# Splitting a weight's high part between ScalarE and GpSimd in a per-sequence-weight FFN kernel

## The reference, cut to what matters

```python
def _L0_cond_ref(x, cat_ids, W, b):
    selected_W = W[cat_ids]
    selected_b = b[cat_ids]
    out = jnp.einsum('bsd,bdh->bsh', x, selected_W) + selected_b[:, None, :]
    return out

def _L0_ffn_ref(x, weight):
    w_scale = jnp.mean(jnp.abs(weight)) + EPS
    u = weight / w_scale
    w_quant = u + jax.lax.stop_gradient(jnp.clip(jnp.round(u), -1.0, 1.0) - u)
    a_scale = jnp.max(jnp.abs(x), axis=-1, keepdims=True) + EPS
    z = jnp.clip(x / a_scale * 127.0, -128.0, 127.0)
    a_quant = z + jax.lax.stop_gradient(jnp.round(z) - z)
    y = jnp.einsum('bsi,oi->bso', a_quant, w_quant)
    y = y * (w_scale * a_scale / 127.0)
    return y
x = x + _L0_ffn_ref(_L0_cond_ref(x, itok_B_0_63, L0_cond_W, L0_cond_b), L0_ffn_weight)
```

## Time and profile before

| what | value |
|---|---|
| median of 3 runs | 501.2 us (500.35 to 503.22) |
| the profiled execution: device time | 501.51 us |
| the profiled execution: span in the trace | 499.5 us |
| TensorE busy | 489.8 us, 98% of the span |
| VectorE busy | 371.3 us, 74% |
| ScalarE busy | 333.4 us, 67% |
| GpSimd busy | 305.9 us, 61% |
| DMA | 172.69 MB, mean 346 GB/s |
| granted TensorE clock | full speed in all 40 slices |

### The profile page before, as it was taken

One profiled execution on the slowest core, in us unless ns is written; L12 is line 12 of the kernel. 1 busy time (PEld: TensorE's weight loads), 2 busy tenths in 40 slices (PEclk: granted clock), 3 DMA queues, 4 the chain that ended last, 5 costly groups with the idle time before them and its releaser, 6 DMA issues.

```text
span 499.5 us, 13165 instructions
## 1 busy us (share of the span) xinstructions
PE 489.8 (98%) x2216; PEld 359.5 (72%) x2217; DVE 371.3 (74%) x653; ACT 333.4 (67%) x503; POOL 305.9 (61%) x399
## 2 busy tenths in 40 slices
PE   8889999999999999999999999999999999999996
PEld 3667777777777777777777777767777777777774
DVE  6658776588866797978757879875989587566844
ACT  3666866677758668868656687666767767567642
POOL 7776665655755656666656656565656665655650
PEclk9999999999999999999999999999999999999999
DMA  7879998999989999999999899979999999799953
GB/s 238 271 265 409 412 302 299 363 364 353 414 292 393 380 413 413 410 404 410 335 305 362 299 406 412 403 273 377 412 382 391 383 387 339 247 359 345 318 160 127
DMA packets 71730, 172.69 MB, mean 346 GB/s; under 512 B 8097, under 2 KB 8354, under 8 KB 71586
## 3 DMA queue, kind: packets, MB, share of 16 engines
q1 hardware_dynamic: 53858, 140.01, 76.4%
q10 hardware_dynamic: 17856, 32.51, 17.4%
HBM read 138.94 MB, written 33.55 MB: 345 GB/s over the span
## 4 chain that ended last, share of the span: by engine, by line
PE 88%; DVE 3%; issue 2%; DMA 2%; POOL 1%; DVEq 1%; SPq 1%; ACT 1%; ACTq 1%; POOLq 0%
PE ps_cond L728 22%; PE ps_cond L730 22%; PE ps_cond L729 21%; PE ps_y L681 20%; PE ps_aT L692 2%; DMA sb_w_raw<-cond_wb 2%; DVE sb_w_lo L566 1%; PE ps_cond L655 1%; DVEq L181 1%; DVE sb_absmax L612 1%; POOL sb_xT_hi L350 0%; POOL sb_xT_lo L355 0%; POOL sb_y_scale L380 0%; ACT sb_aT L467 0%; PE ps_cond L646 0%
## 5 line engine op out<-in xcount | busy, mean ns | idle before, releaser
L355 POOL TENSOR_TENSOR sb_xT_lo<-sb_xT_raw,sb_xT_hi 128x512 fp32r<-128x512 f32 x128 | 191.0, 1492 | 156.7 <-PE ps_cond L730 155.1
L728 PE MATMUL ps_cond<-sb_w_hi,sb_xT_hi 128*128 (+1 forms) x512 | 225.1, 440 | 1.3 <-POOL sb_xT_lo L355 1.3
L730 PE MATMUL ps_cond<-sb_w_hi,sb_xT_lo 128*128 (+1 forms) x512 | 201.4, 393 | 0.0
L729 PE MATMUL ps_cond<-sb_w_lo,sb_xT_hi 128*128 (+1 forms) x512 | 199.4, 389 | 0.0
L612 DVE TENSOR_REDUCE sb_absmax<-ps_cond 128x1 f32<-128x512 f32 x128 | 87.7, 685 | 105.3 <-PE ps_cond L730 98.0
L566 DVE TENSOR_TENSOR sb_w_lo<-sb_w_raw,sb_w_hi x106 | 147.2, 1427 | 0.0
L400 ACT ACTIVATE ps_cond<-sb_w_raw 128x512 f32 x127 | 75.8, 597 | 86.7 <-issue 54.8
L681 PE MATMUL ps_y<-sb_ffnT,sb_aT 128*128 128x512 bf16 x508 | 130.2, 379 | 2.5 <-ACT sb_aT L467 2.4
L486 ACT ACTIVATE sb_a_rounded<-ps_cond,sb_a_inv 128x512 int8<-128x512 f32 x128 | 87.7, 685 | 52.3 <-DVE sb_a_inv L618 51.7
L728 PEld LDWEIGHTS ps_cond<-sb_w_hi,sb_xT_hi 128*128 128x128 f32 x512 | 96.3, 188 | 32.5 <-issue 2.4
L730 PEld LDWEIGHTS ps_cond<-sb_w_hi,sb_xT_lo 128*128 128x128 f32 x512 | 96.1, 188 | 22.4
(11 more groups left out here) (86 smaller groups left out, 46.0 us busy)
## 6 DMA issues: line engine op xcount, KB each, us to landing
sb_w_raw<-cond_wb SPq DMA_DIRECT2D x53, 768.0 KB, 7.4
sb_xT_raw<-x_t SPq DMA_DIRECT2D x128, 256.0 KB, 5.7
sb_x_rows<-x SPq DMA_DIRECT2D x128, 256.0 KB, 5.8
out<-sb_x_rows ACTq DMA_DIRECT2D x124, 256.0 KB, 5.6
sb_w_raw<-cond_wb SPq DMA_DIRECT2D x53, 512.0 KB, 5.4
sb_w_raw<-cond_wb SPq DMA_DIRECT2D x5, 256.0 KB, 3.8
sb_ffn_raw<-ffn_t SPq DMA_DIRECT2D x1, 1024.0 KB, 7.5
out<-sb_x_rows SPq DMA_DIRECT2D x3, 256.0 KB, 2.3
```

The costliest lines, as they stand in the source:

```text
L355: pool.tensor_tensor(xT_lo[:, m, :], xT_raw[:, m, :], xT_hi[:, m, :].bitcast(F32), ALU.subtract).then_inc(x_lo_done, 1)
L728: pe.matmul(ps_cond, x_hi_k, w_hi_k, start=(start and k == 0), stop=False, skip_group_check=True)
L729: pe.matmul(ps_cond, x_hi_k, w_lo_k, start=False, stop=False, skip_group_check=True)
L730: last_mm = pe.matmul(ps_cond, x_lo_k, w_hi_k, start=False, stop=(k == KD - 1), skip_group_check=True)
```

## The change

Of a new step's `w_hi` (2048 columns) ScalarE now makes the first three quarters: its second piece shrinks from 1024 to 512 columns. GpSimd makes the last 512 columns, at the end of its step `r` for step `r+4`, behind `x_hi`. For that it waits for the second DMA of the weight, and it needs the table: it looks up a row at the head of each step, and branches. At the start it does this for steps 1, 2 and 3 ahead of its first step. VectorE's second piece of `w_lo` waits for GpSimd's quarter as well.

```diff
+            def split_last_quarter(new, offset, raw, step, n):
+
+                with pool.If(new > 0):
+                    pool.wait_ge(w_loaded[n], w_landed(step, n))
+                    pool.sem_inc(w_quarter_taken, 1)
+                    pool.tensor_copy(w_hi[:, bass.ds(offset + (W_FREE - H), H)],
+                                     w_raw[:, bass.ds(raw + (W_FREE - H), H)]).then_inc(w_hi_quarter_done, 1)
+                with pool.Else():
+
+                    if type(step) is not int or step > 1:
+                        pool.wait_ge(w_hi_quarter_done, step - 1)
+                    pool.sem_inc(w_hi_quarter_done, 1)
+
+            pool.wait_ge(table_done, 1)
+            for step in range(1, HI_AHEAD):
+                split_last_quarter(*w_raw_slot(pool, step), step, step)
+
             def body(r0, u, first, last):
                 r = r0 + u
 
+                if not last or u + HI_AHEAD < U:
+                    new, offset, raw = w_raw_slot(pool, r + HI_AHEAD)
                 pool.wait_ge(cond_mm_done, r + 1)
...
                     split_x_high(r + X_AHEAD + 1, (u + X_AHEAD + 1) % U)
+                if not last or u + HI_AHEAD < U:
+                    split_last_quarter(new, offset, raw, r + HI_AHEAD, (u + HI_AHEAD) % U)
...
-                        act.activation(w_hi[:, bass.ds(at, PIECE)], w_raw[:, bass.ds(raw + piece * PIECE, PIECE)],
+                        size = PIECE - H if piece == PIECES - 1 else PIECE
+                        act.activation(w_hi[:, bass.ds(at, size)], w_raw[:, bass.ds(raw + piece * PIECE, size)],
                                        ACT.Copy).then_inc(w_hi_done, 1)
...
                         dve.wait_ge(w_hi_done, (step - 1) * PIECES + piece + 1)
+                        if piece == PIECES - 1:
+                            dve.wait_ge(w_hi_quarter_done, step)
```

More of the change, by code:

```diff
@@ L163, in adaln_ffn @@
         w_hi_done = sem("w_hi_done")
+        w_hi_quarter_done = sem("w_hi_quarter_done")
+        w_quarter_taken = sem("w_quarter_taken")
         w_lo_done = sem("w_lo_done")
```

## The result

The changed kernel takes 508.7 us in the median of 5 runs (505.6 to 510.1), the kernel before 502.7 beside it: a ratio of 1.0131, interval 1.0105 to 1.0156, or some 6.6 us more. A second set of runs of the same kernel, further down, gave 1.0123 (1.0088 to 1.0158), 6.2 us. The forecast was 3.8 us over the median of before that was shown. Slower is right and the time lies within the range, but the loss is 1.6 to 1.7 times what the sum gave. The profiled execution took 509.02 us, with a span of 507.3.

What follows compares the result with a forecast made beforehand. TensorE, busy 98% of the span, was taken as the bound. 501.51 us for the profiled execution + 2.5 (start) + 1.3 (other copies) = 505.3, or 505.0 for the median; range 501.6 to 509.

Steps and rivals of the forecast that it cites:

- Terms 1 and 2: At the start, GpSimd's look-ups and first copy make TensorE's step 4 begin late: +2.5 us together, bounds +1.6 to +3.7.
- The chain of look-ups: At the start, GpSimd's four look-ups and three branches between x_hi and x_lo of step 2 take 3.2 us.
- it stands there for about 0.2 us: At the end of its step 0, GpSimd waits about 0.2 us for step 4's weight before the first copy.
- the block by the ternary instruction: At the start, VectorE's ternary instruction and w_lo behind it hold up GpSimd's first copy, which ends at about 24.8 us.
- Term 3: The other 52 copies, in mid-span, cost time where new steps follow each other: +1.3 us, from -1.0 to +2.4.
- six copies of 0.61 us on VectorE's chain are 3.7: In the run of six new steps among 77 to 84, copies add 3.7 us; idle stretches give back about 2.1.
- in a single new step they are hidden: In a lone new step, GpSimd's idle 1.67 us before x_lo and x_lo's 2.5 us lead cover the copy.
- ScalarE's smaller piece at nothing: ScalarE's halved pieces can only remove TensorE's waits for aT: nothing in the sum, up to 1.0 us in the lower bound.
- GpSimd's wait for a weight: In GpSimd's steps, waits for the weight's landing cost nothing: ScalarE's were 6, up to 1.4 us, within 1.7 us free.
- Rival (a): Not slower: the start costs its least and ScalarE's shorter piece removes mid-span waits; 501.8 us (500.9 to 503.7), chance 0.25.
- Rival (b): GpSimd becomes the bound: look-ups don't run beside its work, new steps take 4.4 to 4.7 us; 517 us, chance 0.09.

Runs made afterwards that it cites:

- e12: The change up to step 11 only, from step 12 on as the kernel before: ratio 1.0048 to the kernel before, 2.4 us over.
- e8: Start as the kernel before up to step 11, from step 12 on as the change: ratio 1.0058 to the kernel before, 2.9 us over.
- e3: The change with GpSimd copying 512 unused columns without waiting for a weight, ScalarE making the whole high part: 1.0134 against the kernel before, 6.7 us over.
- e5: As e3, but GpSimd sets the 512 unused columns to zero instead of copying: ratio 1.0083 to the kernel before, 4.2 us over.
- e6: ScalarE makes three quarters, the last is left zero, GpSimd has no look-up or copy: ratio 1.0010 to the kernel before, 0.5 us over.
- e2: The change with GpSimd's look-ups and weight wait but no copy, ScalarE making the whole high part: 1.0016 against the kernel before, 0.8 us over.
- e9: As e8, but GpSimd copies 256 columns instead of 512: ratio 1.0021 to the kernel before, 1.1 us over.
- e4: The change with its first five look-ups moved behind x_lo of steps 2 and 3: ratio 1.0095 to the kernel before, 4.8 us over.
- e10: As e8, but GpSimd copies 768 columns instead of 512: ratio 1.0106 to the kernel before, 5.3 us over.

## Why the prediction was right in direction and short in size

- **Terms 1 and 2 (+2.5 us) were right**: 2.8 us in the trace of the change, 2.4 in e12. Their steps were less so. The chain of look-ups took 3.53 us, not 3.2: a look-up on GpSimd is 737 ns in the median, by VectorE's bound (four of them leave about 0.2 us for each branch, as assumed). And "it stands there for about 0.2 us" was 2.15: the weight of step 4 came later than its row of before said. But the block by the ternary instruction had been counted to 24.4 us anyway, and the copy ended at 25.33 instead of 24.8.
- **Term 3 (+1.3 us) was mis-sized**: e8 measured it alone at 2.9 (1.5 to 4.3), above the forecast's own upper end of 2.4, which the interval takes in; the traced execution of the change lost 5.0. The step that failed is "six copies of 0.61 us on VectorE's chain are 3.7", with "in a single new step they are hidden" ahead of it. I priced the copy by its own duration, in two long runs, and let idle time pay for most of it. In its place e3 against e5 shows that the copy costs by its reads of SBUF, and the trace how: `y_scale`, coming 0.04 us behind a pair of `w_lo` pieces, is held for 2.36 us, then `x_lo` behind the next pair for 2.17, and TensorE waits for it. This happens in short runs too (steps 45 to 47), which I had at nothing. The sum also had no term for TensorE's clock: 1.5 of the 5.0 us.
- **ScalarE's smaller piece at nothing** was right (e6), and so, behind the start, was GpSimd's wait for a weight (e2), though its waits grew to 14, of up to 2.6 us. There TensorE lost time to it only where the copy was there as well.
- **Rival (a)** decided at the copy of step 4, done before 24 us: it was done at 25.33. **Rival (b)** fell: in the steps look-ups run beside the engine's work, and undisturbed steps stay at 3.73 us.
- **Open**: e8 and e12 add up to 5.3 us, the change lost 6.2 and 6.6; the intervals cover that, and no run tells whether the late start adds conflicts. How much of term 3 comes by `x_lo` and how much by `aT` differs from kernel to kernel, and wasn't separated.

None of these versions beats the kernel before; e9, like e2 and e6, is level with it within its interval.

## What to carry to other kernels

Before work is moved off an engine, run the kernel with that work left out: if it is no faster, no placing of the work elsewhere can be. On GpSimd, price an SBUF read by what it meets, not by its length: when VectorE runs two-input instructions back to back, a read that comes just behind the first can stand until the last is done, as `y_scale` did, and so can whatever the new work has delayed.

## What was not expected of the hardware

`y_scale` is not let in between two `w_lo` pieces that follow each other: 19 of these instructions of 0.27 us took about 2.3, the length of both. `x_lo` is let in. Here (DVE, then POOL) it comes as close behind a pair, 0.04 us, and runs between the two pieces, which take 3.42 us instead of 2.35:

```profile
391.36 3.42 DVE L592 TENSOR_TENSOR sb_w_lo<-sb_w_raw,sb_w_hi  x2
...
391.40 2.30 POOL L357 TENSOR_TENSOR sb_xT_lo<-sb_xT_raw,sb_xT_hi 128x512 fp32r<-128x512 f32 x1 [0.49 <-PE ps_cond L756]
```

What makes the difference no run shows.

The clock: behind TensorE's wait of 3.73 us at the start the matmuls of step 2 stand twice as far apart (22.43 and 23.71 above, three matmuls in 1.28 us; 0.69 at full clock), and the same after its waits at 392.28 and 393.94. Stretches of the changed kernel (us, then busy time of PE, PEld, DVE, ACT, POOL; PEclk is the granted clock as a share of 2.4 GHz; DMA share, GB/s):

```profile
16.00:20.00 4.00, 1.18 (x7) 0.93 (x5) 1.70 (x5) 1.19 (x4) 0.49 (x1) 1.00 0.91 287
20.00:24.00 4.00, 3.09 (x10) 2.52 (x11) 3.92 (x5) 2.57 (x4) 1.85 (x4) 0.79 0.88 322
24.00:28.00 4.00, 2.71 (x10) 1.69 (x10) 3.16 (x3) 2.54 (x5) 4.00 (x4) 0.78 0.26 66
28.00:32.00 4.00, 4.00 (x20) 3.01 (x19) 2.28 (x7) 2.64 (x5) 3.69 (x6) 1.00 0.62 196
...
392.00:396.00 4.00, 3.10 (x10) 1.94 (x11) 3.91 (x6) 2.05 (x5) 3.85 (x4) 0.80 0.58 185
396.00:400.00 4.00, 4.00 (x16) 2.96 (x15) 1.90 (x5) 2.01 (x4) 3.07 (x5) 0.77 0.92 277
```

Means of 0.58 to 0.80 are of the two levels, 1.2 and 2.4 GHz. At the start the slow stretch lies mostly ahead of a wait for `x_lo` that TensorE would have had anyway; at 392 us nothing hides it. All 59 runs of the six kernels with look-ups ahead of the first step (the change measured twice) had a mean clock below 0.999, against 30 of 90 of the kernel before, where those 30 took 503.2 us in the median and the other 60 took 501.0. So the slow stretch is part of what the change costs. Where TensorE has no wait the traces show its size: step 4 of e4 takes 5.20 us and step 4 of e10, whose start is that of before, 5.22, instead of 3.65; step 100 of the change takes 5.22 instead of 3.75. That is 1.5 to 1.6 us each. PE and the clock in e10:

```profile
27.71 0.79 PE L757 MATMUL ps_cond<-sb_w_hi,sb_xT_hi 128*128 x1
...
32.93 0.58 PE L757 MATMUL ps_cond<-sb_w_hi,sb_xT_hi 128*128 x1
...
28.00:32.00 4.00, 4.00 (x12) 3.14 (x12) 1.36 (x4) 2.04 (x4) 2.46 (x4) 0.61 0.73 180
```

How much of the ratios in the table is the clock's no run takes by itself.
